# A macaron block of windowed and global attention: another order of one round's steps on four engines

## What is computed

```python
x = x + 0.5 * ffn(layernorm(x))          # ffn: 2 layers of local attention + gated MLP
x = x + attn(layernorm(x)) @ weight      # 16 heads, queries = keys, over all 512 tokens
x = x + 0.5 * ffn(layernorm(x))
```

```python
h = shift_token(x); q, k, v = split(h @ wqkv)          # 256 -> 3 x 512
q = l2norm(q) * qs; k = l2norm(k) * ksc; q, k = rotary_xpos(q, k)
x = x + local_attention(q, k, v) @ wo                  # own window and the one before
h = shift_token(x); h = (h - mean) / sqrt(var + 1e-5) * lg + lb
a, g = split(h @ w1 + b1)                              # 256 -> 2 x 682
x = x + (a * gelu(g)) @ w2 + b2
```

## Time and profile before

| | |
|---|---|
| timed runs | 3995.21, 3997.68, 4005.38 us |
| the profiled execution | 3996.88 us, of which 3995.2 us are the span of its instructions |
| mean granted clock of TensorE | 0.987 |
| busy: PE, DVE, ACT, POOL | 94%, 64%, 56%, 55% of the span |
| chain that ended last: PE, DVE, issue, POOL | 80%, 10%, 4%, 2% |

### The profile page before, as it was taken

One profiled execution on the slowest core, in us unless ns is written; L12 is line 12 of the kernel. 1 busy time (PEld: TensorE's weight loads), 2 busy tenths in 40 slices (PEclk: granted clock), 3 DMA queues, 4 the chain that ended last, 5 costly groups with the idle time before them and its releaser, 6 DMA issues.

```text
span 3995.2 us, 75738 instructions
## 1 busy us (share of the span) xinstructions
PE 3743.9 (94%) x23552; PEld 3057.5 (77%) x23552; DVE 2572.0 (64%) x7286; ACT 2228.2 (56%) x5232; POOL 2182.8 (55%) x2175
## 2 busy tenths in 40 slices
PE   4999999999999799999999999998999999999997
PEld 2777777777777688888888888776777777777776
DVE  6776677766776455565555655556676677766774
ACT  2655665566556455444444444445655665566554
POOL 3565555555555355565555555554565556555653
PEclk9999999999999899999999999999999999999999
DMA  4010001100110100000000010001000011100110
GB/s 141 16 31 25 18 18 52 54 29 24 34 37 19 51 27 17 1 17 16 3 17 2 17 44 1 17 1 51 20 31 25 18 41 49 45 24 24 34 31 25
DMA packets 119045, 114.53 MB, mean 29 GB/s; under 512 B 13180, under 2 KB 116232, under 8 KB 118792
## 3 DMA queue, kind: packets, MB, share of 16 engines
q1 hardware_dynamic: 118792, 111.44, 8.9%
HBM read 73.69 MB, written 29.36 MB: 26 GB/s over the span
## 4 chain that ended last, share of the span: by engine, by line
PE 80%; DVE 10%; issue 4%; POOL 2%; DMA 1%; ACT 1%; SPq 1%; DVEq 0%; POOLq 0%; ACTq 0%
PE psum L1347 20%; PE psum L1348 18%; PE psum L1349 18%; PE psum L1459 6%; PE psum L1489 5%; PE psum L1469 5%; PE psum L1594 3%; PE psum L1448 2%; DVE nrm L1107 2%; DVE nrm L1105 1%; PE psum L1542 1%; DMA nrm<-xmid 1%; PE psum L1507 1%; DVE turned_qk L1015 1%; PE psum L1427 1%
## 5 line engine op out<-in xcount | busy, mean ns | idle before, releaser
L674 POOL TENSOR_TENSOR ge_lo<-ge,ge_hi 128x512 fp32r<-128x512 f32 x512 | 716.9, 1403 | 560.2 <-PE psum L1349 305.6
L634 POOL TENSOR_SCALAR probs<-probs,rz 128x256 f32<-128x256 f32 (+1 forms) x1024 | 444.6, 454 | 505.3 <-DVE rz L1067 505.3
L872 ACT ACTIVATE ge<-psum 128x512 f32<-128x512 f32 x512 | 306.3, 598 | 635.4 <-PE psum L1594 635.4
L1239 DVE CAST ge_hi<-ge 128x512 fp32r<-128x512 f32 x512 | 243.7, 478 | 560.5 <-ACT ge L872 558.4
L778 ACT ACTIVATE probs<-probs,nb,rq 128x256 f32<-128x256 f32 (+1 forms) x1024 | 575.9, 566 | 42.0 <-DVE nb L1061 41.2
L1053 DVE CUSTOM_DVE_ANT_0 probs<-psum,mask 128x256 f32<-128x256 f32 (+1 forms) x1024 | 339.1, 387 | 275.4 <-PE psum L1459 275.4
L624 POOL TENSOR_TENSOR rinv<-ssq,minus_half 128x16 f32<-128x16 f32 x128 | 378.6, 2958 | 161.6 <-DVE ssq L1030 157.7
L1347 PE MATMUL psum<-wqkv_hi,hT_hi 128*128 128x512 f32 x768 | 333.2, 434 | 54.8 <-DVE turned_sin L1019 53.3
L759 ACT ACTIVATE squares<-psum 128x512 f32<-128x512 f32 x256 | 150.2, 599 | 351.9 <-PE psum L1349 224.8
L644 POOL TENSOR_TENSOR hid_lo<-gate,hid_hi 128x512 fp32r<-128x512 f32 x160 | 207.5, 1297 | 254.0 <-ACT hid_hi L810 254.0
L1348 PE MATMUL psum<-wqkv_hi,hT_lo 128*128 128x512 f32 x768 | 306.5, 399 | 0.0
(11 more groups left out here) (162 smaller groups left out, 10558.5 us busy)
## 6 DMA issues: line engine op xcount, KB each, us to landing
xnext<-stream SPq DMA_DIRECT2D x32, 512.0 KB, 4.5
xmid<-stream SPq DMA_DIRECT2D x32, 512.0 KB, 3.8
stream<-xmid SPq DMA_DIRECT2D x16, 512.0 KB, 2.9
nrm<-xmid SPq DMA_DIRECT2D x32, 224.0 KB
wbuf<-L_ffn_wqkv SPq DMA_DIRECT2D x8, 768.0 KB, 9.0
wbuf<-L_ffn_w SPq DMA_DIRECT2D x8, 682.0 KB, 4.1
x_all<-L_attn_x SPq DMA_DIRECT2D x8, 512.0 KB, 7.6
stream<-x_all SPq DMA_DIRECT2D x8, 512.0 KB, 3.9
```

Source lines behind the costliest of these rows:

```text
L634: last = nc.gpsimd.tensor_scalar(pu, pu, rz[:, h, t:t + 1], 1.0, ALU.mult, ALU.mult)
L674: nc.gpsimd.tensor_tensor(ges[1][:, k % 4, :], ge[:, k % 4, :], f32(ges[0][:, k % 4, :]), ALU.subtract).then_inc(S["g_lo"], 1)
L872: nc.scalar.activation(ge[:, k % 4, :], RB[k % 2], ACT.Exp, scale=GSCALE, accum_out=gz[:, h, t:t + 1]).then_inc(S["g_exp"], 1)
```

## The change

The four tables are written in another order. All steps are the same, with the same waits of their own; the bank waits of PE follow from its new table. `PE_DRAIN`, `ACT_DRAIN` and the `AHEAD_*` tables stay.

```diff
-PE_STEPS = ("S0 -g3 -a2 S1 -w0 -a3 S2 -g4 T0 S3 -w1 T1 S4 -a4 -w2 T2 A0 S5 A1 T3 S6 -w3 T4 S7 A2 A3 +z0 +z1 -w4 "
-            "-g5 T5 +q0 +k0 A4 T6 +k1 -w5 +q1 A5 W0 T7 A6 +q2 W1 A7 +Q0 +k2 +K0 W2 W3 B +K1 +k3 +Q1 +q3 +Q2 +v0 "
-            "+v1 +v2 n0 n1 +v3 +Q3 g0 a0 +K2 g1 a1 +K3 g2").split()
-ACT_STEPS = ("-G2 -G3 E0 -u2 E1 i0 E2 i2 H0 -G4 H1 E3 i1 -u3 H2 E4 O0 H3 E5 -u4 E6 H4 O1 +zh0 +zh1 E7 -G5 +sq0 H5 "
-             "-u5 +sk0 H6 +sq1 +sk1 H7 O2 f0 +sq2 O3 f1 +Qc0 +Kc0 +sk2 +sk3 +Qc1 +sq3 +vh0 +vh1 +Qc2 +Kc1 nh0 nh1 "
-             "G0 f2 +vh2 +vh3 +Qc3 +Kc2 u0 G1 +Kc3 u1").split()
-DVE_STEPS = ("X0 -y2 X1 R0 X2 i0 R1 L0 X3 i2 -y3 R2 L1 -y4 X4 i1 R3 L2 X5 R4 L3 X6 X7 P0 R5 L4 P1 R6 +zl0 +zl1 L5 "
-             "-y5 +rq0 R7 +rk0 L6 +ss0 -F -e +rk1 +ss1 +rq1 L7 +c0 P2 f0 P3 f1 +rq2 +c1 +rk2 x +ss2 l +rk3 r +rq3 "
-             "j +ss3 nl0 nl1 B +c2 y0 f2 +Y +c3 y1").split()
-POOL_STEPS = ("-ul1 N0 -ul2 N1 N2 N3 -ul3 N4 -ul4 N5 N6 -ul5 N7 +d0 +p0 +b0 +p1 +b1 +d1 +b2 +d2 +p2 s +b3 +d3 +p3 "
+PE_STEPS = ("S0 -g3 S1 -a2 -w0 S2 -a3 T0 -g4 S3 -a4 T1 S4 -w1 T2 S5 A0 -w2 A1 T3 S6 A2 A3 T4 S7 -w3 +z0 +z1 -w4 "
+            "-g5 T5 +k0 +q0 T6 A4 +q1 -w5 +k1 A5 W0 T7 W1 A6 +q2 A7 +k2 +Q0 W2 W3 B +K0 +k3 +K1 +q3 +Q1 +v0 +Q2 "
+            "+v1 +v2 n0 n1 +v3 +Q3 g0 a0 g1 +K2 a1 +K3 g2").split()
+ACT_STEPS = ("-G2 -G3 E0 E1 i0 -u2 E2 i2 H0 -G4 H1 E3 i1 -u3 H2 E4 O0 H3 -u4 E5 O1 E6 H4 +zh0 +zh1 E7 -G5 +sk0 H5 "
+             "-u5 +sq0 +sq1 +sk1 H6 O2 f0 H7 +sq2 O3 f1 +sk2 +Kc0 +Qc0 +sk3 +Qc1 +sq3 +Kc1 +vh0 +vh1 +Qc2 nh0 nh1 "
+             "G0 f2 +vh2 +vh3 G1 +Kc2 u0 +Qc3 +Kc3 u1").split()
+DVE_STEPS = ("X0 X1 -y2 R0 X2 i0 R1 -y3 L0 X3 i2 R2 -y4 L1 X4 i1 R3 X5 L2 R4 L3 X6 X7 P0 R5 L4 P1 +zl0 +zl1 R6 R7 "
+             "L5 -y5 +rk0 L6 +rq0 +ss0 -F -e +rk1 +ss1 +c0 L7 +rq1 +c1 P2 f0 P3 f1 +rq2 +ss2 x +rk2 l +rk3 r +rq3 "
+             "j +ss3 nl0 nl1 B +c2 y0 f2 +c3 y1 +Y").split()
+POOL_STEPS = ("-ul1 N0 -ul2 N1 N2 N3 N4 -ul3 -ul4 N5 N6 N7 -ul5 +d0 +b0 +p0 +d1 +p1 +b1 +b2 +d2 s +d3 +b3 +p2 +p3 "
```

## The result

| | before | changed |
|---|---|---|
| median of 6 runs each (lowest to highest) | 3997.60 us (3995.21 to 4005.38) | 4019.89 us (4014.96 to 4025.05) |
| ratio, 95% interval | | 1.0051 (1.0040 to 1.0062) |
| the profiled execution, its span | 3996.88, 3995.2 us | 4022.33, 4020.6 us |
| mean granted clock of TensorE | 0.987 | 0.985 |

The change costs 22 us, 0.5%, and the interval does not reach 1: the kernel is slower. The forecast was no change, 4000 us, with a chance of 0.48 for a difference within 0.3% and 0.32 for slower. It was 20 us too low; the range of 3984 to 4025 held the time, and only because it reached to the end of a rival whose reckoning was another one (see the part on the prediction).

The account below looks back on a forecast made before the run. PE, busy 94%, was taken as the bound, with DVE's x-to-j chain in the middle stretch. Layer 0 rounds 0, layer 1 +0.7 us, start and ends +2: together +3, 4000 us, no change; range 3984 to 4025.

Parts of the forecast that it names:

- What bounds the kernel: Layer 0 round: PE's own work sets the outer two stretches, a DVE chain from x to j the middle one.
- First stretch: S0 to the end of W3, layer 0: K0 -0.36, borders +0.2, S1's wait +0.05; sum -0.1 us a round.
- K0's -0.36: K0 moved from before W2 to behind W3, where PE has time to spare: saves 0.36 us per round.
- Nothing is added: T0 comes 9.05 us after S0, N0 ends at 9.02: no cost, but 1.3 us of slack gone.
- n0 to S0: Last stretch of a layer 0 round, 10.92 us: PE busy throughout, no wait should turn up.
- Middle: W3 to n0: r waits for the shift DMAs, j is late by +0.1 us a round (-0.2 to +0.3).
- Layer 1: Up to W3: W0's wait on e stays because L6 joins the chain to e; -0.05 us a round.
- The faster rival: W0's wait on e goes, saving 0.65 us in 14 rounds, plus cheaper borders: 3984 us; chance 0.2.
- p2 beside j: Power p2 on POOL, now beside j on DVE, costs nothing; by the Skill's rule n0 would be 2.9 us later.
- The start: Nothing covers p2 and p3 there, p3 right behind p2: up to 2.9 us once, taken as 1.
- The slower rival: Lost slack: a late H5 delays T6 and all up to W3, 0.5 to 0.9 us in 29 rounds: 4013 to 4024; chance 0.28.
- T6 behind H5: Sign of the slower rival: T6 waits on H5 every round; the main reckoning had no wait, 0.15 us to spare.

Follow-up runs that it names:

- e10_t0: The changed kernel with g4 ahead of T0 again on PE; 4010.34 us, ratio 1.0033 to the kernel before.
- e8_first_joined: The kernel before with the new order only up to z, R6 and R7 ahead of the rotary products on DVE; 4007.80 us, ratio 1.0024 to the kernel before.
- e9_d2: The changed kernel with a second buffer for the keys' sine product; 4009.08 us, ratio 1.0023 to the kernel before.
- e6_t6: The changed kernel with A4 ahead of T6 and rq0 ahead of L6 again; 4006.82 us, ratio 1.0017 to the kernel before.
- e12_best: e11_best with A4 ahead of T6 and rq0 ahead of L6; 3978.68 us, ratio 0.9955 to the kernel before.
- e5_p2: The changed kernel with the power p2 ahead of s again on POOL; 4011.60 us, ratio 1.0027 to the kernel before.
- e7_second_joined: The kernel before with the new order only from z on, N7 ahead of ul5 on POOL; 3996.78 us, ratio 0.9993 to the kernel before.
- e11_best: e7_second_joined with the second sine buffer, K0 ahead of the biases and p2 ahead of s; 3990.72 us, ratio 0.9972 to the kernel before.

## Where the prediction was right and where it was wrong, step by step

The range held by luck. The sum was +3 us and the change measured +22: half of that is the start and the first round, which the sum had at 1 us and at nothing; 7 to 12 us are the steady rounds, which it had at 0 and +0.05 us and which are 0.4 longer; the rest lies in the rounds and the stage that scatter, and stays open.

**What bounds the kernel**: right. PE's own row of steps up to W3, and behind it the chain from x to j on DVE. Everything measured in a steady round fits in these two.

**First stretch, -0.1 forecast, +0.26 measured. This step failed.** K0's -0.36 was right (-0.35). "Nothing is added" at T0 was wrong: N0 ended when I said, but T0 starts only 0.14 us behind it; I had set N0's end (9.02) against PE's arrival (9.05) with no release between, and the only release I had priced was 0.05 from DVE. e10_t0 prices T0's new place at 0.17. S1 was right: it starts 2.57 us after S0, a wait of some 0.04. The waits at first matmuls, as g5's for P1, and the two new pieces make the rest of +0.62. I had counted borders and looked only at waits that I expected; where all slack is gone, each release showed, at 0.05 to 0.15 us. e8_first_joined shows the sum, +0.60.

**n0 to S0, unchanged forecast:** right (10.89 after 10.92).

**Middle, +0.1 forecast, +0.18 measured: right in size, wrong in the reason.** "r waits for the shift DMAs", so rk2 behind x is free, holds only with two buffers (e9_d2). I had named q3's wait on rk2, which came, and missed d2: rk3 writes the buffer that d2 reads.

**Layer 1: right in what binds, wrong in size.** The forecast was +0.05 us a round with the wait on e kept; the wait stayed (0.56 us), and the round grew by 0.40. F comes 0.5 us later where I had 0.3, because the delay of the first half, forecast as -0.1, is handed on through A4 and L6; the middle stretch grew by 0.27, not 0.1, and e9_d2 takes that back (12.04 us). The wait on e stays because L6 was put ahead of rq0 and A4 behind T6: e6_t6 takes it away by undoing that, and e12_best again. The faster rival was therefore nearly right about the sum at stake (it had 0.65 us in 14 rounds, and 0.47 came back), wrong that the change sets it free. Undone together with T6 and A4, it is not shown which of the two swaps does it; the row of L6, 0.85 us idle until A4, says both are in it.

**p2 beside j: right.** Six operations of j lie beside p2 at 0.33 us and e5_p2 leaves the rounds as they are. By the rule of the Trainium skill (SBUF — State Buffer, who interferes with whom), by which one excludes the other for its whole length, they would have been held for up to 2.92 us; for the power it does not hold. With POOL's rotations it agrees: the two operations of j beside d3 and b3 take 1.3 us, as long as d3 and b3 themselves. F, which is no TENSOR_SCALAR, takes 2.48 us beside b0 and 1.32 beside the power p0.

**The start, +1 forecast, +3.9 measured; the first round, not in the sum, +6.8. This step failed as well.** I looked at p2 alone, and it is 1.6 us (e5_p2), near the 1 I took. What I left out is k2 ahead of Q0: with no steps of another batch between, it waits 1.53 us and runs at the lower clock, and Q0 is 4.3 us late. I did not cost the first round at all; there too PE has nothing to fill its waits, and it is longer with either half of the new order, partly by the clock. These 10.7 us are half of the whole loss. The 1 us for the last rounds of the calls did not show: they changed by +0.6 and -0.7.

**The slower rival** gave the right time, 4013 to 4024, by a mechanism that for the most part did not occur. Of its two signs, T0 behind N0 came in nearly every round, at 0.14 us; T6 behind H5, on which its 0.5 to 0.9 us in 29 rounds rested, did not, and the start and the first round, half of the 22 us, were no part of it. T6 comes at 524.36, H5 ended at 524.24, and k0 with q0 ahead of T6 took 2.86 us, where q0 with k0 had taken 2.96 ahead of A4: it was not held up. The slack that was gone was T0's. That its time fits is luck. It deserved the larger chance; "three near ties where there was slack of a microsecond" was the better guide than the reckoning that found each of them just in time.

## What to carry to other kernels

Where an order is changed so that a step arrives just in time, add the 0.05 to 0.15 us that a release took here, and ask for each moved write which reader of its buffer moved with it. Cost the first round on its own: what is hidden in a steady round is bare there, and PE may run at the lower clock. And do not judge half of an order by running it alone before its joints to the other half are checked: here two halves that cost 57 and 25 us cost 10 and nothing once a step or two were moved in each. Nor do good halves make a good whole: these two save 0.1 to 0.2 us each in a round of layer 1, and together they cost 0.4, because one makes PE late and the other hands the delay on.

## What was not expected of the hardware

- The same kind of POOL instruction, TENSOR_TENSOR, blocks DVE in one place and not in another. The rotations (128x512) make a TENSOR_SCALAR of 0.33 us last 1.3, and two SCALAR_TENSOR_TENSORs last 2.48 instead of 1.32; beside a power of 128x16 elements, 2.9 us long, DVE's operations keep their 0.33 us. Whether the operation (an addition, a power) or the size makes the difference is not shown.
- A release of PE takes 0.14 to 0.17 us from POOL (end of N0 to T0, in 31 of 32 rounds of the changed kernel) and 0.05 from DVE (P1 to g5).
- Where PE has no other batch's work between its waits, its clock can go down from 2.4 to 1.2 GHz, and the waits at the place do not tell whether it does. At the start it went down behind a wait of 2.25 us for 6.8 us in the changed kernel, and around one of 2.50 us for 3.4 us in the kernel before. In the first round, behind waits of 1.13 and 2.14 us in the same order of steps, it stayed up in e7_second_joined and was down for 3.4 us in e11_best.
